# Cross attention's probabilities: split to fp16 halves first, turned by crossbar DMA transposes instead of TensorE

## The reference

```
x = x + self_attention(layernorm(x))         # 16 heads of 32, causal, a rotation on q and k
x = x + cross_attention(layernorm(x), ctx)   # q: 100 rows, k and v: 722 rows, 16 heads of 32
x = x + moe(layernorm(x))                    # 8 experts of 512x512, the best 2 per token

# cross attention, for each sequence and head
attn = softmax((q * scale) @ k.T)            # 100 x 722
out  = attn @ v                              # 100 x 32
```

## Time and profile before

| | |
|---|---|
| runs | 1573.17 us median of 3 (1571.85 to 1574.92) |
| profiled execution | 1579.41 us, its span 1577.6 us |
| TensorE busy | 1445.2 us, 92% of the span |
| VectorE busy | 1069.5 us, 68% |
| ScalarE busy | 688.4 us, 44% |
| GpSimd busy | 372.1 us, 24% |
| granted TensorE clock, mean | 0.957 |
| mean DMA rate | 57 GB/s |

### The profile page before, as it was taken

One profiled execution on the slowest core, in us unless ns is written; L12 is line 12 of the kernel. 1 busy time (PEld: TensorE's weight loads), 2 busy tenths in 40 slices (PEclk: granted clock), 3 DMA queues, 4 the chain that ended last, 5 costly groups with the idle time before them and its releaser, 6 DMA issues.

```text
span 1577.6 us, 36390 instructions
## 1 busy us (share of the span) xinstructions
PE 1445.2 (92%) x14004; PEld 1025.0 (65%) x14004; DVE 1069.5 (68%) x1926; ACT 688.4 (44%) x1336; POOL 372.1 (24%) x490
## 2 busy tenths in 40 slices
PE   4789999999999999999899999999996789999999
PEld 4467777677776777777777777677775644444444
DVE  4658878687868786887778686878876654333332
ACT  4335555465646554655556464655554410000000
POOL 1522314132232323231323133232312200000000
PEclk9999999999999999999999999999997689999999
DMA  8133140404041322314040404132224010000002
GB/s 245 28 72 69 37 96 11 100 7 99 16 91 34 71 62 45 85 26 95 12 99 7 100 8 98 35 71 65 46 61 138 1 42 27 28 27 27 27 0 84
DMA packets 82914, 90.41 MB, mean 57 GB/s; under 512 B 32428, under 2 KB 68580, under 8 KB 82748
## 3 DMA queue, kind: packets, MB, share of 16 engines
q1 hardware_dynamic: 82748, 88.05, 23.3%
HBM read 41.06 MB, written 6.55 MB: 30 GB/s over the span
## 4 chain that ended last, share of the span: by engine, by line
PE 64%; DVE 14%; issue 7%; ACT 5%; POOL 4%; SPq 4%; DMA 2%; DVEq 0%; POOLq 0%; ACTq 0%
PE psum L258 42%; PE psum L764 7%; PE psum L742 4%; PE psum L753 4%; DVE c_max L988 3%; SPq L576 3%; DVE s_sum L1050 2%; ACT prob L852 2%; PE psum L696 1%; DVE c_raw L938 1%; POOL c_raw L1192 1%; PE psum L672 1%; DVE probT L996 1%; POOL x_norm L1137 1%; DMA arena<-in_L_attn_Wv 1%
## 5 line engine op out<-in xcount | busy, mean ns | idle before, releaser
L988 DVE TENSOR_REDUCE c_max<-psum 100x1 f32<-100x722 f32 x256 | 231.7, 905 | 81.3 <-PE psum L742 74.8
L858 ACT ACTIVATE probT<-psum 121x600 f16<-121x600 f32 x256 | 171.6, 670 | 262.7 <-PE psum L764 262.1
L852 ACT ACTIVATE prob<-psum,c_bias 100x722 f32<-100x722 f32 x256 | 219.9, 859 | 40.0 <-DVE c_bias L991 39.5
L764 PE MATMUL psum<-ident,prob 100*121 100x100 f32 x1536 | 232.9, 291 | 0.0
L996 DVE TENSOR_TENSOR probT<-psum,probT 121x600 f16<-121x600 f32 x256 | 199.1, 778 | 27.4 <-ACT probT L858 22.6
L258 PE MATMUL psum<-w_kv,cT 128*121 128x512 f16 x864 | 199.8, 380 | 0.0
L258 PE MATMUL psum<-cT,w_kv 128*128 128x361 f16 x1152 | 197.1, 318 | 0.0
L764 PEld LDWEIGHTS psum<-ident,prob 100*121 100x121 f32 x1536 | 195.8, 197 | 0.1
L481 DVE SCALAR_TENSOR_TENSOR w_self_all<-psum,g_now,w_self_all 128x512 f32<-128x512 f32 x104 | 77.8, 750 | 168.5 <-PE psum L258 168.4
L742 PE MATMUL psum<-arena,stack_q 96*100 96x361 f16 x512 | 130.0, 336 | 35.0 <-ACT prob L852 31.4
L258 PEld LDWEIGHTS psum<-w_kv,cT 128*121 128x121 f16 x864 | 112.9, 135 | 59.4 <-issue 0.5
(11 more groups left out here) (160 smaller groups left out, 2086.5 us busy)
## 6 DMA issues: line engine op xcount, KB each, us to landing
arena<-split_k SPq DMA_DIRECT2D x192, 180.5 KB, 3.9
c_raw<-in_ctx SPq DMA_DIRECT2D x16, 907.5 KB
stack_q<-split_qk SPq DMA_DIRECT2D x192, 25.0 KB, 1.9
split_k<-in_L_ffn_expert_w SPq DMA_DIRECT2D x4, 1024.0 KB, 5.2
cv<-in_L_ffn_expert_w SPq DMA_DIRECT2D x4, 1024.0 KB, 5.2
x_in<-in_x SPq DMA_DIRECT2D x16, 200.0 KB
x_scratch<-x_mid SPq DMA_DIRECT2D x16, 200.0 KB
w_self_all<-x_scratch SPq DMA_DIRECT2D x12, 256.0 KB, 5.8
```

The lines of the kernel that those rows point to most:

```text
L764: last = pe.transpose(pT[0:CW, t // 3, (t % 3) * L:(t % 3 + 1) * L], prob[h % 2][:, t * CW:(t + 1) * CW], ident[0:L, 0:L])
L852: act.activation(prob[h % 2][:, 0:LC].rearrange("q (a k) -> q a k", a=2), score[0:L, :, 0:HC], ACT.Exp, bias=c_bias[:, int(odd), h:h + 1], ...
L858: act.activation(probT[:, 0].rearrange("k (a c) -> k a c", a=2), pT[0:CW, :, 0:3 * L], ACT.Copy)\
L988: dve.tensor_reduce(c_max[:, int(odd), h:h + 1], score[0:L, :, 0:HC], AXIS.XY, ALU.max)\
```

## The change

The probabilities are no longer turned by TensorE in fp32.

- ScalarE casts `prob` (100 x 722, SBUF) to the high half, in its own layout, into `prob16`; GpSimd, no longer VectorE, subtracts for the low half. `prob16` has 112 rows (the 12 behind 100 are zero) and 2 x 768 columns per head, and two buffers, by the head's parity.
- SyncE then issues one `dma_start_transpose` per head, both halves in one (112 x 1536 fp16), into `probT`, again two buffers. It waits for the low half of its head and for the output of the head two before. The cast of a head waits for the transpose of the head two before, and the exp of a head for the low half of the head two before.
- In step h stand the scores of head h (before: h+1) and the output of head h-3 (`LAG`; before: h-1). The scores of head 0 move from step 15 to step 0 of the next iteration.
- Key tiles are 128 rows instead of 121, the last one 82; the padding of the context goes.
- The outputs of four heads have a PSUM bank each time, and their sum runs behind the seventh, eleventh and fifteenth step and in step 2 of the next iteration. TT and TP move from steps 3 and 4 to 5 and 6, other chunks move with them.
- GpSimd and SyncE now go by steps. GpSimd's other work stands ahead of the low half of its step: rotations in steps 1 to 3, the scaling of the heads in 4, shifts in 5 and 6, scalings in 7 and 8, the normalization of x_mid in 12, the split of the queries in 14, the normalization of x_in in 15. SyncE's copies of keys stand in steps 13 and 14 (six each), those of queries in step 15 (groups 0 and 1) and step 0 of the next iteration (groups 2 and 3), each ahead of its step's transpose.

```diff
 STEP_CHUNKS = [
     ["X1T", "CX0", "SQ"],
-    ["CX1", "SK"],
-    ["CX2", "CX3", "SV"],
-    ["CX4", "CX5", "TT"],
-    ["SS0", "SS1", "TP"],
-    ["SS2", "SS3", "CK0"],
-    ["CV0", "CK1"],
-    ["SP0", "SP1", "CK2"],
-    ["SP2", "SP3", "CK3"],
-    ["CK4", "SO"],
-    ["CK5", "OP"],
-    ["CK6", "CK7"],
-    ["X2T", "CV1", "CQ"],
-    ["CV2", "CV3"],
+    ["CX1", "SK", "CX2"],
+    ["CX3", "SV"],
+    ["CX4", "CX5", "CK0"],
+    ["CK1", "SS0", "SS1", "CK2"],
+    ["TT", "CK3", "SS2", "SS3"],
+    ["TP"],
+    ["CV0", "CK4"],
+    ["SP0", "SP1", "CV1"],
+    ["SP2", "SP3", "CK5"],
+    ["SO", "CK6"],
+    ["OP"],
+    ["CK7", "CV2"],
+    ["X2T", "CV3", "CQ"],
     ["CV4"],
     ["CV5"],
 ]
-PE_ORDER = "0SOT123"
-ACT_ORDER = "0PE123"
+PE_ORDER = "0SO123"
+ACT_ORDER = "0E1H23"
...
+        def turn_probs(sp, n, h):
+
+            g = H * n + h
+            if not (isinstance(g, int) and g < 2):
+                wait_alone(sp, head_done, g - 1)
+            wait_alone(sp, prob_low, g + 1)
+            sp.dma_start_transpose(out=probT[h % 2], in_=prob16[:, h % 2].rearrange("q p k -> q (p k)"))\
+              .then_inc(prob_turned[h % 2], 16)
...
+            for h in range(H):
+                if h == 0 and it.cross:
+                    wait_alone(sp, cq_split, m)
+                    for c in range(2, HT):
+                        stack_queries(sp, it.odd, c)
...
+                if it.prep:
+                    if h == 13:
+                        if it.tail:
+                            wait_alone(sp, score_ready, H * n)
+                        wait_alone(sp, chunk_out, it.done(f"CK{2 * KD - 1}"))
+                    if h in (13, 14):
+                        for c in range(2 * (h - 13), 2 * (h - 12)):
+                            stack_keys(sp, odd_m, c)
+                    if h == 15:
+                        wait_alone(sp, cq_split, m + 1)
+                        for c in range(2):
+                            stack_queries(sp, odd_m, c)
...
+                if it.cross:
+                    turn_probs(sp, n, h)
...
         def pe_head_out(pe, n, odd, h):
-            pe.wait_ge(pT_out, H * n + h + 1)
+            g, group = H * n + h, 4 * n + h // 4
+            if h % 4 == 0 and not (isinstance(group, int) and group < 2):
+                pe.wait_ge(heads_summed, group - 1)
+            pe.wait_ge(prob_turned[h % 2], 16 * (H // 2 * n + h // 2 + 1))
...
-        def pe_transpose_probs(pe, n, h):
-            g = H * n + h
-            pe.wait_ge(exp_done, g + 1)
-            if not (isinstance(g, int) and g < 1):
-                pe.wait_ge(pT_out, g)
-            for t in range(CT):
-                last = pe.transpose(pT[0:CW, t // 3, (t % 3) * L:(t % 3 + 1) * L],
-                                    prob[h % 2][:, t * CW:(t + 1) * CW], ident[0:L, 0:L])
-            last.then_inc(pT_ready, 1)
...
         def act_exp(act, n, odd, h):
+            g = H * n + h
+            if not (isinstance(g, int) and g < 2):
+                act.wait_ge(prob_low, g - 1)
...
         def act_probs_high(act, n, h):
-            act.wait_ge(pT_ready, H * n + h + 1)
-            act.activation(probT[:, 0].rearrange("k (a c) -> k a c", a=2), pT[0:CW, :, 0:3 * L], ACT.Copy)\
-               .then_inc(pT_high, 1)
+            g = H * n + h
+            if not (isinstance(g, int) and g < 2):
+                act.wait_ge(prob_turned[h % 2], 16 * (H // 2 * n + h // 2))
+            act.wait_ge(exp_done, g + 1)
+            act.activation(prob16[0:L, h % 2, 0, 0:LC], prob[h % 2][:], ACT.Copy).then_inc(prob_high, 1)
...
-        def dve_probs_low(dve, n, h):
-            dve.wait_ge(pT_high, H * n + h + 1)
-            return dve.tensor_tensor(probT[:, 1].rearrange("k (a c) -> k a c", a=2), pT[0:CW, :, 0:3 * L],
-                                     probT[:, 0].rearrange("k (a c) -> k a c", a=2), ALU.subtract)
...
+        def pool_probs_low(pool, n, h):
+
+            pool.wait_ge(prob_high, H * n + h + 1)
+            pool.tensor_tensor(prob16[0:L, h % 2, 1, 0:LC], prob[h % 2][:], prob16[0:L, h % 2, 0, 0:LC],
+                               ALU.subtract).then_inc(prob_low, 1)
```

More of the change, by code:

```diff
@@ L36 @@
 CT = 6
-CW = 121
-LCP = CT * CW
+CW = 128
+CLAST = LC - (CT - 1) * CW
 HC = LC // 2
-HP = LCP // 2
+HP = CT * CW // 2
+PR = 112
+PT = 2 * CT * PR
+LAG = 3
 TT = (T + P - 1) // P
@@ L549, in sync_iteration @@
+        def turn_probs(sp, n, h):
[5 more added lines that the diff above has]
+              .then_inc(prob_turned[h % 2], 16)
         def sync_iteration(sp, it):
             n, m = it.n, it.n + 1
-            if it.tail:
-                wait_alone(sp, chunk_out, it.done("TP"))
-                sp.dma_start(x2_dram[n - 1], x_mid[1 if not it.odd else 0][:]).then_inc(x2_stored, 16)
-                if isinstance(n, int) and n == B - 1:
-                    sp.wait_ge(head_done, H * n)
-                    load_expert(sp, 1, 1)
-                    load_y(sp, EARLY - 1)
-                elif isinstance(n, int) and n == B:
-                    for t in range(EARLY, TT):
-                        load_y(sp, t)
@@ L583, in sync_iteration @@
-            if isinstance(n, int) and n == B - 2:
-                for c in range(HT):
-                    sp.wait_ge(k_stacked[c], 16 * 3 * B)
-                sp.wait_ge(chunk_out, it.done("OP"))
-                load_expert(sp, 0, 0)
-                sp.dma_start(g_raw, gW).then_inc(g_loaded, 16)
-                for t in range(EARLY - 1):
-                    load_y(sp, t)
-                sp.wait_ge(g_loaded, 16)
-                sp.dma_start(e_bias, eb).then_inc(g_loaded, 16)
+            odd_m = not it.odd
@@ L1151, in pool_split_q, with pool_rotate @@
             return pool.tensor_tensor(split_qk[:, QLOW], tmp_q[:], split_qk[:, QHIGH], ALU.subtract)
+        def pool_rotate(pool, it, which, part):
+            name = ("SQ", "SK")[which]
+            count = 2 * (it.n + 1) + which
+            tmp, high, low = ((tmp_q, QHIGH, QLOW), (tmp_k, KHIGH, KLOW))[which]
+            rotation = rope_t[:].unsqueeze(1).to_broadcast([P, KD, L])
+            if part == 0:
+                pool.wait_ge(chunk_out, it.done(name))
+                if which == 0 and not (isinstance(it.n, int) and it.n < 0):
+                    for c in range(HT):
+                        pool.wait_ge(cq_stacked[c], 16 * 3 * (it.n + 1))
+                pool.tensor_tensor(split_qk[:, high], tmp[:], rotation, ALU.mult).then_inc(qk_high, 1)
+            elif part == 1:
+                pool.wait_ge(qk_high, count + 1)
+                pool.tensor_tensor(tmp[:], tmp[:], rotation, ALU.mult).then_inc(qk_rotated, 1)
+            else:
+                pool.wait_ge(qk_rotated, count + 1)
+                pool.tensor_tensor(split_qk[:, low], tmp[:], split_qk[:, high], ALU.subtract).then_inc(qk_split, 1)
```

311 lines of the change are left out of this document (163 added, 148 removed).

## The result

The kernel after takes 1730.97 us in the median of 4 runs (1726.12 to 1732.12), the kernel before 1572.89 (4 runs beside it): ratio 1.0976 [1.0929, 1.1023]. The change makes it slower by 158 us; the forecast was +41 (1614), with a range of 1540 to 1780. The side was right and the size was off by almost four times.

What follows compares the result with a forecast made beforehand. TensorE was taken to bound iterations 0 to 14. Period 75.1 for 73.1 us gave +30, the last attention iteration +5.7, its end +5: +41, so 1614 us; range 1540 to 1780, the forecast's own 1590 to 1680.

Steps and rivals of the forecast that it cites:

- The seam: Between two iterations, head-0 scores wait for query copies behind key copies and three transposes: 9.2 us of TensorE idle.
- X2T: X2T waits for GpSimd's normalization of x_mid behind low half 11: 2.0 us idle, plus 0.9 for the exp loop.
- SP0: In step 8, SP0 waits for GpSimd's scaling behind low half 6: 1.3 us idle.
- The clock: After the seam's idle, TensorE's next stretch starts at the lower clock level: 2.0 us in each iteration.
- the sum of waits that made the period 75.1: Per iteration: 57.2 us of TensorE work plus 15.9 idle gives 73.1, plus 2.0 for the clock.
- T = 1.6 us: SyncE's time for one 344 KB crossbar transpose, taken from the key copies' rate; ends kept at 0.3 and 7.2.
- Of the present 3.8 us idle, 2.0 are of other kinds and stay: TensorE's existing idle per iteration outside the changed waits stays at 2.0 us.
- short steps: Steps with less than the exp loop's 3.16 us of TensorE work: 0.5 us idle an iteration.
- The end terms: Outside the fifteen periods: last attention iteration +5.7 us, its end +5, setup 0.
- the two-deep buffers: Cast of head h+2 waits for transpose h: at least 3.9 us a head, 50.7 us where 52.7 are left.
- Rival 1: Slow transpose: from landing about 6.5 us the buffers bound every head; 1790 us at 8, chance 0.20.
- Rival 3: Transposes at plain-copy speed beyond the key copies', T = 1.0 and landing 4 us: 1585 us, chance 0.10.

Runs made afterwards that it cites:

- e2: The kernel after with only its chunks reordered, CX4 and CX5 apart from CK0 and SO apart from SP3: 1713.08 us, ratio 1.0868.
- e1: The kernel after with the query copies of groups 0 and 1 moved ahead of the second six key copies and transpose 14: 1705.29 us, ratio 1.0846.
- e4: The kernel after with e1's and e2's edits joined, key copies one step earlier and all query copies in steps 14 and 15: 1718.65 us, ratio 1.0923.
- e7: e4 taken further: keys computed by step 9 and copied in steps 10 to 13, both normalizations ahead of GpSimd's low half: 1693.62 us, ratio 1.0742.
- e13: e8 with 6 instead of 36 unread products ahead of X1T: 1586.40 us, ratio 1.0078.
- e6: e1 plus unread products filling TensorE's waits (36 ahead of X1T, 20 CK0, 14 X2T, 12 SO): 1684.41 us, ratio 1.0696.
- e9: e8 with GpSimd's low half working on only 8 of 722 columns: 1583.58 us, ratio 1.0044.
- e8: e6 with each crossbar transpose replaced by a plain DMA of 112 rows x 224 bytes: 1594.52 us, ratio 1.0105.
- e14: e6 with all transposes and 6 instead of 36 unread products ahead of X1T: 1669.65 us, ratio 1.0598.
- e12: e6 with each transpose turning the high half only (172 KB for 344 KB): 1649.9 us, ratio 1.0457.
- e5: The kernel after with unread products filling TensorE's waits ahead of X1T, head-0 scores, CK0, X2T and SO: 1726.55 us, ratio 1.0957.

## Why the prediction was right in sign and wrong in size

**Right.** TensorE is rid of its 11 us (59.56 us busy at the mixed clock; 57.2 and 2.0 for the clock had been forecast). The seam is where the queue's order put it: TensorE runs dry 10.7 us after X2T starts (forecast 10.9), X1T starts at 14.6 (14.9), the scores wait for the query copies. X2T waits 2.07 (2.0), SP0 1.10 (1.3). The cast takes 0.80 (0.77) and the low half 1.56 (1.70). The clock sinks behind the seam.

**The step that failed is the sum of waits that made the period 75.1.** It is 82.6 from head 0 to head 0. By its terms, in the iteration of 81.8 above, 6.3 of the 6.7 us missing are idle time: 22.2 for 15.9.

- *The seam: 12.3 for 9.2.* "T = 1.6 us" was taken from the key copies' rate and used three times beside them. The three cost 2.59, 2.30 and 1.89, 6.8 in all for 4.8. Small gaps between the entries of SyncE's list, forecast as none, add 1.1 (0.06 to 0.38 each); the key and query copies are 0.4 over the forecast. These 3.5 us are 3.1 of idle time, since X1T itself ran 0.93 for 0.35 at the lower clock and TensorE ran dry 0.2 earlier. T is 1.37 on a free queue, better than forecast, and there lay the fault: one number for a cost that has two. The DMA engines' time grew by (924 - 368) / 256 = 2.17 us for each transpose. As an estimate, three of them are 6.5 us of the 20.6 us (0.93 x 22.1) that the engines were busy at the seam. That the engines' share of 0.26 "leaves room" was read from an iteration's mean; in the very stretch where the transposes were to go it was 0.93 already.
- *"Of the present 3.8 us idle, 2.0 are of other kinds and stay": 6.2.* CK0 2.98, SO 2.01, SQ 0.47, OP 0.49, a score 0.24. The diff moves CX5 right in front of CK0, and SO ahead of its neighbour; I took the new order of the chunks as neutral. e2 took up CK0's wait and most of SO's and gave 18 us.
- *Terms that were too high:* X2T 2.6 with its exp loop (2.07 and 0.52) for 2.9, SP0 1.1 for 1.3, and short steps nothing for 0.5.
- *The mean over iterations* is 0.8 above the undisturbed ones, the spread that the kernel before has as well.
- *The clock: 59.56 busy for 57.2 and 2.0.* The size came out, but by luck, for the 2.6 us between the two iterations of the earlier trace rows aren't the price of a clock spell. TensorE's busy time differs by 1.07 (69.30 for 68.23). The other 1.5 is idle time: the longer iteration holds a turn of the loop, at which X1T waits 3.10 us where it waits 1.56 otherwise:

```profile
605.45 0.93 PE L629 MATMUL psum<-ident,x_norm 100*128 100x100 f32 x4 [3.10 <-issue]
```

The end terms sum to +3.0 (5.2 and -2.2) for +10.7, an error the other way. The heads of the last attention iteration are 3.4 us apart, not the 3.85 that the two-deep buffers were to allow (nine of them from 1366.68 to 1397.41): with 3.5 us to landing for the 5.0 of the sum, that bound is (0.80 + 1.56 + 0.3 + 3.5) / 2 = 3.1.

**What the experiments add** is that no one term is "the" cause. Seven edits (e1, e2, e4 to e7, e13) were expected, by taking their waits off the sum, to bring 60 to 200 us each, and brought 4 to 37: behind each wait stood the next. In e1, e4, e6 and e7 the next wait was mostly that of the casts, 165 to 181 us of it. A cast waits for the transpose two heads back, ScalarE is in order, so the next exp and the scores behind it wait too; the bound that I had put at 3.9 us a head and let go with "it holds by little" is broken where landings are late. The largest single part is the transposes: 74 us in the kernel as it is, 90 with the seam open, 34.5 for half the bytes. About 19 are GpSimd's. With no transposes, no low half, the seam opened and the clock held (e9) the order still only draws with the old one, 1.0044, with the fillers' overrun in it. What holds this last part is not settled. In e13 each wait is short (X1T 3.3, SP0 1.1, CK0 0.8, SO 0.7, X2T 0.5, a head's output 1.1), and I tried neither an order drawn up afresh without transposes, nor more than two buffers, nor the context's load in another step.

**The rivals.** Rival 1 (landing so late that the buffers bound every head) was right in its mechanism and wrong in its place: alone a transpose lands in 3.5 us, but behind the context's load in 8.0, beside the key copies in 4.4 to 5.9 (the transposes from 564.29 to 584.52). Most of the casts' 84.2 us of waiting falls to heads 13 and 15 (67.4), which wait for these. Its threshold was also set too high: by the text's own two lines, 50.7 us for 13 heads where 52.7 are left, the buffer bound takes over from X about 5.3, not 6.5. Rival 3 leaned on a rate. By the Trainium skill ("Advanced Engine Details and Errata", X-Bar Transpose (TRN2)) transposing DMAs are as fast as plain ones; this trace disagrees: 344 KB in 2.17 us of all 16 engines is 158 GB/s. The key copies of the kernel before moved 200 GB/s with the engines at 0.93, which is 215 GB/s of busy time.

## What to carry to other kernels

When work moves from a full engine to DMA, add up the DMA engines' time in the stretch where transfers already bunch, not over the whole iteration (0.26 looked like room; during the key copies it was 0.93 before the change). Give an operation two prices, alone and beside its neighbours, and run the sum with the dearer one where they meet. Don't take one iteration for all of them either: five iterations here hold a turn of the loop, and two readings went wrong by it, that of the earlier trace rows and that of e8. And don't add up the waits of a schedule as what their removal is worth: with buffers two deep and engines in order, the eight edits e1, e2, e4 to e7, e13 and e14 gave 6 to 37% of what had been expected of them.

## What the runs showed of the hardware

- A crossbar transpose of 112 x 1536 fp16 from SBUF to SBUF holds SyncE for 1.37 us and lands 3.5 us after issue (medians); of 112 x 768, 1.21 and 2.6. Right behind a load of 960 KB it took 3.10 and 8.0 us, beside the key copies 1.89 to 2.59 and 4.4 to 5.9.
- It moves in small pieces: (434908 - 82748) / 256 = some 1376 packets each. 12 x 112 = 1344 of them would be rows of 256 bytes; the other 32 I can't place. e12 has some 704, 672 and the same 32. This agrees with the Trainium skill ("DMA: Bandwidth & Descriptors", SDMA does more than copy), which has the transpose work on tiles of 256 bytes.
- GpSimd's subtraction of 100x722 (fp32 and fp16 in, fp16 out) takes 1.56 us, 2.15 ns a column, less than the 2.36 that 400 columns cost.
- TensorE's granted clock rose from 0.88 to 0.97 by products that nobody reads (e5), and the kernel gained 4 us from it, within the noise; with the seam opened it rose from 0.89 to 0.95 (e6) and the kernel gained 21.
- At each turn of the loop of two iterations TensorE idles with no releaser recorded: 2.9 to 3.2 us in the kernel before, 1.4 to 2.4 of them after X1T's input was there.
